# First tile projected ahead of the weights' sums, gate and up weights converted on GpSimd and ScalarE, rows added behind the first gated block, high halves of the last down projection first

## The reference

```python
xn = layernorm(x)                                  # x: 4 x 1024 x 256, no gain or bias
q, kv = xn @ Wq, xn @ Wkv                          # 256 x 256 each, 16 heads of 16
q, kv = rotary(q) * DH ** -0.5, rotary(kv)         # the keys are the values too
attn = softmax(q @ kv.T)                           # per head, 1024 x 1024
a = (attn @ kv) @ Wout + bout
h = silu(xn @ wg.T) * (xn @ wu.T)                  # wg, wu: int32 * (1/127), 768 x 256
f = h @ wd.T                                       # wd: int32 * (1/127), 256 x 768
out = x + a + f
```

## Time and profile before

| | |
|---|---|
| median of 3 runs | 826.01 us (825.84 to 827.42) |
| profiled execution | 825.99 us, its span 824.1 us |
| TensorE busy | 796.4 us (97%) |
| VectorE busy | 743.5 us (90%) |
| ScalarE busy | 691.3 us (84%) |
| GpSimd busy | 272.5 us (33%) |
| granted TensorE clock | 1.00 |

### The profile page before, as it was taken

The page is one execution under the profiler, slowest core; times in us unless marked ns, Lnnn a source line. Parts: engine busy times, 40 slices in busy tenths (PEclk is TensorE's granted clock), DMA queues, the critical chain, the costliest instruction groups (busy, mean ns, idle before and its releaser), DMA issues.

```text
span 824.1 us, 19134 instructions
## 1 busy us (share of the span) xinstructions
PE 796.4 (97%) x7316; PEld 295.5 (36%) x7316; DVE 743.5 (90%) x893; ACT 691.3 (84%) x1270; POOL 272.5 (33%) x502
## 2 busy tenths in 40 slices
PE   4998999998999999999999999999999999999997
PEld 2354555554323333333333333333333333333234
DVE  5898888887999999999999999999999999999702
ACT  5665555545999999999999999999999999999982
POOL 3797888885020100001222222222222222222210
PEclk9999999999999999999999999999999999999999
DMA  9666554445011111112112222122222122222322
GB/s 311 146 151 149 128 117 109 108 104 122 23 30 36 31 31 30 32 39 52 50 49 54 56 57 50 50 53 53 55 58 54 49 51 53 59 53 51 87 70 74
DMA packets 111680, 60.55 MB, mean 73 GB/s; under 512 B 71372, under 2 KB 101900, under 8 KB 111588
## 3 DMA queue, kind: packets, MB, share of 16 engines
q1 hardware_dynamic: 111588, 59.32, 28.5%
HBM read 28.57 MB, written 16.90 MB: 55 GB/s over the span
## 4 chain that ended last, share of the span: by engine, by line
PE 85%; POOL 4%; ACT 3%; DVE 3%; issue 3%; DMA 1%; SPq 0%; DVEq 0%; ACTq 0%; POOLq 0%
PE ps L756 33%; PE ps L773 18%; PE ps L738 15%; PE ps L633 7%; PE ps L647 3%; ACT arena L1018 2%; POOL arena L1348 1%; DVE negmax L1180 1%; DMA arena<-w_up_dram 1%; PE ps L610 1%; PE ps L612 1%; PE ps L611 1%; PE ps L682 1%; PE ps L784 1%; POOL side L1339 1%
## 5 line engine op out<-in xcount | busy, mean ns | idle before, releaser
L1180 DVE TENSOR_REDUCE negmax<-ps 128x2 f32<-128x1024 f32 x512 | 588.9, 1215 | 6.2 <-PE ps L773 5.8
L1018 ACT ACTIVATE arena<-ps 128x512 f32<-128x512 f32 x1024 | 555.3, 595 | 31.8 <-PE ps L738 10.0
L756 PE MATMUL ps<-arena 128*32 128x256 f32 x4072 | 326.5, 392 | 2.4 <-issue 2.2
L738 PE MATMUL ps<-qs,ks 51*128 51x512 f16 x1024 | 197.8, 382 | 3.3 <-ACT arena L1018 2.1
L773 PE MATMUL ps<-ks,qs 48*128 48x512 f16 x972 | 189.4, 386 | 0.1
L756 PEld LDWEIGHTS ps<-arena 128*32 128x32 f32 x4072 | 80.4, 107 | 128.3 <-issue 127.2
L773 PEld LDWEIGHTS ps<-ks,qs 48*128 48x128 f16 x972 | 46.5, 92 | 195.5 <-DVE negmax L1180 143.4
L1453 POOL TENSOR_TENSOR arena<-arena,x_all 128x256 f32<-128x256 f32 x22 | 16.0, 728 | 230.4 <-ACT arena L1039 230.4
L633 PE MATMUL ps<-arena,side 128*128 128x512 f16 x384 | 88.9, 380 | 3.3 <-DVE side L1125 3.3
L738 PEld LDWEIGHTS ps<-qs,ks 51*128 51x128 f16 x1024 | 50.7, 93 | 77.1 <-ACT arena L1018 43.6
L1382 POOL TENSOR_TENSOR mparts<-rowmax,munit 128x16 f16<-128x16 f32 x32 | 7.1, 222 | 210.4 <-DVE rowmax L1190 210.4
(11 more groups left out here) (118 smaller groups left out, 519.2 us busy)
## 6 DMA issues: line engine op xcount, KB each, us to landing
parts_d<-arena SPq DMA_DIRECT2D x64, 128.0 KB
x_all<-x_dram SPq DMA_DIRECT2D x8, 512.0 KB, 8.9
qs<-parts_d SPq DMA_DIRECT2D x64, 64.0 KB, 1.9
ks<-parts_d SPq DMA_DIRECT2D x64, 64.0 KB, 1.9
o_d<-arena SPq DMA_DIRECT2D x124, 32.0 KB
arena<-o_d SPq DMA_DIRECT2D x24, 128.0 KB
arena<-inv_d SPq DMA_DIRECT2D x48, 64.0 KB
out_dram<-arena SPq DMA_DIRECT2D x24, 128.0 KB, 1.8
```

The lines of the kernel that those rows point to most:

```text
L738: mm = pe.matmul(ps[:, score_bank(place(p, kt, 2 * half + a)), :], ks[ring][top:top + ROWS, kt * P:(kt + 1) * P], qs[ring][top:top + ROWS, ...
L756: mm = pe.matmul(ps[32 * j:32 * j + 32, 7, cols], vstage[pl % 2][:, j % 2, kt, :], probs[PER_STEP * (kt % PBUF) + j][:, cols], start=(kt = ...
L1018: act.activation(probs[PER_STEP * (kt % PBUF) + j], ps[:, score_bank(place(p, kt, j)), :], ACT.Exp).then_inc(exp_done, 1)
L1180: dve.tensor_reduce(negmax[pl % 2][:, h, :, kt], ps[:, bank:bank + 2, :], AX.X, ALU.max, negate=True).then_inc(max_done, 1)
```

## The change

Five edits, all in the first phase. (1) project(0) no longer waits for the sums of the weights' maxima: the small sum matmul is placed between its tiles 0 and 1, each half of the transposed rows is waited for by itself, and ScalarE makes both fp32 copies before the fp16 ones. (2) The gate weights are converted on GpSimd instead of VectorE, the up weights on ScalarE (behind high_x(1)) instead of GpSimd. (3) The four add_ffn of a chunk stand behind gated(c, 0) instead of before it. (4) From chunk 1 on, GpSimd's keep_values stands behind low_hid(c, 1) instead of ahead of low_hid(c, 0). (5) The last down projection takes all high halves of the four tiles first, then the low halves; only the second group waits for GpSimd.

```diff
@@ TensorE
+            def sum_maxima():
+                pe.wait_ge(ones_set, 1)
+                pe.wait_ge(wmax_done, 2)
+                pe.matmul(ps[:, 7, 0:2], onesf[:, :], wmax[:, :], start=True, stop=True).then_inc(wsum_done, 1)
+
             def project(c):
                 if c:
                     pe.wait_ge(x_turned, 32 * c)
                 else:
-                    pe.wait_ge(xT_copied, 2 * KD)
+                    pe.wait_ge(wqkv_in, 32)
...
+                    if c == 0 and t == 1:
+                        sum_maxima()
                     for k in range(KD):
+                        if c + t == 0:
+                            pe.wait_ge(xT_copied, k + 1)
...
                     pe.wait_ge(xl_ready, KD)
                     pe.wait_ge(wg_ready, 1)
-                    pe.wait_ge(wud_ready, 1)
+                    pe.wait_ge(wu_ready, 1)
...
-            def down_most(c, t):
+            def down_high(c, t):
                 if t == 0:
                     pe.wait_ge(hh_done, KH * (c + 1) - 1)
-                    pe.wait_ge(hl_done, KH * (c + 1) - 1)
                     pe.wait_ge(y_done, CT * c)
                 elif t == 2:
                     pe.wait_ge(silu_done, KH * (c + 1))
                     pe.wait_ge(hid_done, KH * (c + 1))
-                for n in range(2 * (KH - 1)):
-                    hp = (hh, hl)[n // (KH - 1)]
-                    k = n % (KH - 1)
-                    pe.matmul(bank_down(c, t), hp[:, k, t * P:(t + 1) * P], wd[:, k, :], start=(n == 0), stop=False)
+                for k in range(KH - 1):
+                    pe.matmul(bank_down(c, t), hh[:, k, t * P:(t + 1) * P], wd[:, k, :], start=(k == 0), stop=False)
+
+            def down_low(c, t):
+                if t == 0:
+                    pe.wait_ge(hl_done, KH * (c + 1) - 1)
+                for k in range(KH - 1):
+                    pe.matmul(bank_down(c, t), hl[:, k, t * P:(t + 1) * P], wd[:, k, :], start=False, stop=False)
...
             turn_first_x()
-            pe.wait_ge(wqkv_in, 32)
-            pe.wait_ge(ones_set, 1)
-            pe.wait_ge(wmax_done, 2)
-            pe.matmul(ps[:, 7, 0:2], onesf[:, :], wmax[:, :], start=True, stop=True).then_inc(wsum_done, 1)
...
             for t in range(CT):
-                down_most(last, t)
+                down_high(last, t)
+            for t in range(CT):
+                down_low(last, t)
@@ ScalarE
                 act.activation(xnT[:, k, :], bank_x(k), ACT.Copy).then_inc(xT_copied, 1)
+
+            def high_first_x(k):
                 act.activation(xh[0][:, k, :], bank_x(k), ACT.Copy).then_inc(xT_copied, 1)
+
+            def whole_up():
+                act.wait_ge(ints_in[1], 16)
+                act.activation(wu[:, :, :], int_u, ACT.Copy).then_inc(wu_ready, 1)
...
             for k in range(KD):
                 copy_first_x(k)
+            for k in range(KD):
+                high_first_x(k)
...
                     high_x(c + 1)
+                if c == 0:
+                    whole_up()
@@ VectorE
-            dve.wait_ge(ints_in[0], 16)
-            dve.tensor_copy(wg[:, :, :], int_g).then_inc(wg_ready, 1)
             for c in range(NCHUNK):
                 rope_chunk(c)
                 if c == 1:
                     moments(3 * CT, 3)
+                gated(c, 0)
                 if c:
                     for t in range(CT):
                         add_ffn(c - 1, t)
-                gated(c, 0)
@@ GpSimd
-            for w, of, i in ((wu, int_u, 1), (wd, int_d, 2)):
-                pool.wait_ge(ints_in[i], 16)
-                pool.tensor_copy(w[:, :, :], of).then_inc(wud_ready, 1)
+            pool.wait_ge(ints_in[0], 16)
+            pool.tensor_copy(wg[:, :, :], int_g).then_inc(wg_ready, 1)
+            pool.wait_ge(ints_in[2], 16)
+            pool.tensor_copy(wd[:, :, :], int_d).then_inc(wd_ready, 1)
...
-                keep_values(c)
                 if c == 0:
+                    keep_values(0)
                     low_x(1)
                 for j in range(KH):
                     low_hid(c, j)
+                    if c and j == 1:
+                        keep_values(c)
```

More of the change, by code:

```diff
@@ L227, in build @@
         wg_ready = sem("wg_ready")
-        wud_ready = sem("wud_ready")
+        wu_ready = sem("wu_ready")
+        wd_ready = sem("wd_ready")
         stats_done = sem("stats_done")
@@ L639, in down @@
                 if t == 0:
-                    pe.wait_ge(wud_ready, 2)
+                    pe.wait_ge(wd_ready, 1)
                     pe.wait_ge(hh_done, KH * (c + 1))
@@ L1098, in low_first_x @@
             def low_first_x(k):
-                dve.wait_ge(xT_copied, 2 * (k + 1))
+                dve.wait_ge(xT_copied, KD + k + 1)
                 dve.tensor_tensor(xl[0][:, k, :], xnT[:, k, :], xh[0][:, k, :], ALU.subtract).then_inc(xl_ready, 1)
             def low_first_qk(t):
-                dve.wait_ge(wud_ready, 1)
+                dve.wait_ge(wu_ready, 1)
                 dve.wait_ge(qk_hi_done, t + 1)
@@ L1343, in low_qk @@
                 if c == 0 and t == 0:
-                    pool.wait_ge(wud_ready, 2)
+                    pool.wait_ge(wu_ready, 1)
                 elif t == 0:
```

## The result

The changed kernel takes 828.26 us (median of 12 runs, 826.85 to 829.82) against 826.05 (12 runs, 825.37 to 827.90): ratio 1.0024, 95% interval 1.0016 to 1.0032, which is 2.0 us slower (1.3 to 2.6; the two medians lie 2.2 apart). The prediction was 829.1, slower. Its profiled execution took 826.85, with a span of 825.1, so it is one of the quicker ones of the changed kernel, and 0.86 above the profiled execution of before.

A forecast was written before the change was run, and what follows sets the result against it. TensorE was taken to bound nearly the whole span, with VectorE and GpSimd setting the pace in the first 37 us. 0.9 - 0.2 - 0.5 + 0.4 + 2.4 + 1.3 - 1.2 = +3.1 gave 829.1, range 826.8 to 830.4.

The forecast's parts named there:

- +0.4, three times +0.8 and +1.3: Chunks 3 to 7: additions queued behind gated(c, 0) delay the first maximum; TensorE waits once per chunk, bounds 0 to +6.7.
- Forecast -1.2: Last down projection: it starts once the high half is there, 196.8 instead of 198.09; -1.2, bounds 0 and -1.3.
- Forecast -0.7: Chunks 1 and 2: TensorE waits shrink as low halves precede the copy of the values; -0.2 and -0.5.
- the term "+0.9": Start: gated(0, 0) comes at 27.9 instead of 27.00; +0.9, bounds -0.2 and +1.5.
- the second half waits for the conversion: Start: the second low half waits for GpSimd's down-weight conversion, so tile 0's rotation begins at 19.9 against 18.21.
- rival (a): Start: the second low half gets ahead of GpSimd's down-weight conversion; start -0.2, sum +2.0, 828.0; chance 0.20.
- rival (b): Start: TensorE's faster pace comes sooner, ratio meets the gate conversion; start -1.1, sum +1.1, 827.1; chance 0.10.
- The 8.0 from the first rotation to gated(0, 0): Start: 8.0 is left of 8.8, as the bias rows and the wait for TensorE's tile no longer delay it.
- "same": Whole kernel: chance 0.20 of no telling change, from the rest of (a), (b) and most of (c).
- (c): Chunks 3 to 7: the waits don't appear, as TensorE has hidden slack; sum -1.0, 825.0; chance 0.08.
- both low halves colliding: Start: both low halves meet GpSimd, at the conversion and the bias rows; 829.9 given, within a more-waiting rival of chance 0.15.

The follow-up runs named there:

- e2: Changed kernel with the additions behind gated(c, 0) in chunks 1 and 2 only, before it from chunk 3 on: 823.25 us, ratio 0.9965.
- e1: Kernel before with edit 3 alone, the four additions behind gated(c, 0) in every chunk: 830.69 us, ratio 1.0049.
- e3: Kernel before with edit 5 alone, high halves of the last down projection first: 825.76 us, ratio 0.9986.
- e11: Changed kernel with edit 3 undone in all chunks: 822.77 us, ratio 0.9956.
- e12: Changed kernel with edit 4 undone, keep_values ahead of the low halves again: 828.10 us, ratio 1.0021.
- e8: Changed kernel again, unchanged, for a second profile and more executions: 827.85 us, ratio 1.0022; its profiled execution took 827.90.
- e7: Changed kernel with the sums' matmul again in front of tile 0: 827.77 us, ratio 1.0017.
- e6: Changed kernel with additions before gated(c, 0) from chunk 3 on, and GpSimd converting the down weights only after the low halves: 824.01 us, ratio 0.9976.
- e4: Kernel before with edits 1 and 2 alone (start and conversions): 826.81 us, ratio 1.0001.
- e9: Changed kernel with the statistics of chunk 1 taken off the way to project(0): 827.46 us, ratio 1.0016.

## Why the prediction was right, and where it was not

**Chunks 3 to 7, edit 3: right, by mechanism and size.** Forecast +0.4, three times +0.8 and +1.3, 4.1 in all. The waits of the changed kernel are 0.31, 0.73, 0.74, 0.74 and 1.26, 3.8 in all, and by the marks the stage lost 4.06 (e2). The chunks are 23.3 apart instead of 22.49, as forecast. e1 and e2 show the cause from both sides: the edit alone costs 4.0, taking it back from chunk 3 on makes the kernel faster than the one before. gated(c, 0) could not come earlier, as it waits for silu(c, 0); the additions had filled that gap for nothing.

**Edit 5: right.** Forecast -1.2; e3 measured -1.2 (-1.9 to -0.5), and 1.3 by the marks of its profile.

**Chunks 1 and 2, edits 3 and 4: the sum was right, the shares only in part.** Forecast -0.7, by the marks -0.6: 0.05 in chunk 1, where I had 0.2, and 0.57 in chunk 2, where I had 0.5. TensorE's wait of 1.04 in chunk 1 shrank to 0.62 one block later, and the 1.31 in chunk 2 became 0.80 one unit sooner, as the prediction had it. But e11 and e12 show that all of the win is edit 4's: alone it shortens the stage by 57.9 - 56.8 = 1.1, alone edit 3 by nothing (57.9 in e1, 58.0 in e12), together they win 0.6. So in chunk 2 as well the additions take back 0.5.

**Edits 1 and 2: the term "+0.9" was wrong.** The step that failed is "the second half waits for the conversion: 17.8 + 1.46 + 0.64 = 19.9". In no profile did it wait. In e8 TensorE kept the slow pace as I had assumed and the sums started at 15.05, my 15.0; still the low halves began at 16.92 and not at 17.15, the second one at about 17.6, and the conversion came at 18.77 and not at 17.72. From the sums to the ratio it was 0.71 there instead of the 0.99 that I had carried over. That part follows the pace of the two sum records: 0.56 for them gives 0.99 (before, e7), 0.43 gives 0.85 (e6), 0.28 gives 0.71 or 0.72. I had taken the landing of the down weights at 17.72 as fixed, and it is not. So rival (a) is what happened, by mechanism and nearly by size: it had the second low half ahead of the conversion, a start of -0.2 and 828.0, and e8 shows -0.3 and 827.90.

In the first profile rival (b) came on top, in part: TensorE's pace rose within tile 0, which I had held hardly possible, so the sums came at 14.27 although project(0) started 0.2 later than the 11.5 of the sum (11.72). The low halves were over at 17.43, the 17.4 of (b), and the start won 1.2 against its 1.1. But (b) had the ratio meet the gate conversion, and that was over at 13.22.

The 8.0 from the first rotation to gated(0, 0) was too short as well: it is 8.44 in the first profile and 8.54 in e8, since additions of chunk 0 still stand beside GpSimd's bias rows (0.82 and 1.10 instead of 0.68).

In the median the start is worth +0.1 (e4, -0.8 to +0.9), which leaves room for the -0.3 of e8. What the runs show is that the new start depends more on when the rows of chunk 1 land. With the landing at 8.5 to 9.1 (VectorE's first statistics of those rows), gated(0, 0) came at 25.2 to 26.7 in seven profiles of the new start, against 27.00 before. With a landing at 10.63 it came at 28.47 (e6), while the old start had it at 27.35 with one at 9.91 (e1) and at 27.78 with one at 10.36 (e3). Old: 0.8 later for a landing 1.45 later (e3); new: 2.7 later for 1.6. Two things differ. The slow pace of tile 0 now stands in front of the sums (1.0 of the 2.7). And in e3 the first rotation was 1.5 later too, but 0.7 of it came back before gated(0, 0), most of it by the wait of 0.36 for TensorE's tile, which was gone, and a shorter addition (0.89 for 1.11). Each is read from one or two profiles. e9 shows that the path runs through VectorE's statistics and ScalarE's roots. Since all stages behind gated(0, 0) repeat, the spread of the profiled executions comes from the start. What stays open is how often the rows land late in executions that aren't profiled, and what else spreads them: in e9 the spread is 2.2, and its interval does not exclude that it changed nothing in the median.

**The total.** Forecast +3.1, measured +2.0 (1.3 to 2.6). By the marks of e8: start -0.3, chunks 0 to 2 -0.6, chunks 3 to 7 with the last down projection +2.8, together +1.8; with e4's +0.1 for the start it would be +2.3. So nearly the whole miss is the start term, 0.9 where the runs show between -0.3 and +0.1. That the kernel is slower was forecast for the right reason, edit 3. That 828.26 still lies in the stated range owes nothing to the start: its term had the wrong sign in both profiles, and the result is nearer to rival (a)'s 828.0 than to 829.1, just outside the 828.5 to 829.7 that the forecast had given itself. Two small sums of the prediction don't work out either: its 0.20 for "same" holds 0.03 of the 0.08 of (c), not most of it, and both low halves colliding would give 829.7, not 829.9.

## What to carry to other kernels

Work that fills a wait is free only in its place. Before moving an operation behind another, look at what the other waits for, and at what then stands behind the moved one: here 1.3 us of additions left a gap of 1.2 and landed in front of a maximum that the bounding engine was about to need. And read a start not from one execution: an order that wins when a load lands early can lose when it lands late, if it puts a slow stretch behind that load.

## What the runs showed of the hardware

TensorE's pace in the first tile differed between executions of the same kernel with the same work in front: four fp32 records in 2.71 us in the first profile of the changed kernel, in 3.43 in the second, while the twelve records behind the sums took 5.40 both times (weight loads 0.43 apart, against 0.86 at the slower pace). In one execution the rise from 1.2 to 2.4 GHz fell into tile 0, in the other at its end. The granted clock is given as 0.998 and 0.997 for the whole of the two, and as 1.00 for the 3.5 us of slow loads in the second: here the spacing of the weight loads shows the pace, and the column of the clock does not. Where such a rise falls in front of a chain of small waits, the first execution shown is no measure of the others.

A VectorE operation of 128x1 with both inputs in SBUF took 1.27, 1.24 and 1.30 us (before, e1, e3) where GpSimd was converting, and each time ended within 0.02 of the conversion's end. It took 0.16 in every profile in which the conversion was over, in e7 too, where the order of the sums is the old one.

ScalarE converted 1536 int32 columns to fp16 in 1.47 us, the same as GpSimd's 1.46, where I had allowed up to 1.7.
